# Cross-attention softmax denominators: one quad of each head summed by VectorE, with its neighbours' shares moved between GpSimd and TensorE

## The reference

```python
h, d, M = 16, 32, 8192
q = (layernorm(x) @ Wq + bq)        # 512 tokens, 16 heads of 32
k, v = ctx @ Wk + bk, ctx @ Wv + bv # 8192 keys
scores = einsum('nhd,mhd->hnm', q, k) / sqrt(32)
attn = softmax(scores, axis=-1)     # exp / sum over the 8192 keys
out = einsum('hnm,mhd->nhd', attn, v)
x = x + relu(out @ W1 + b1) @ W2 + b2
```

## Time and profile before

| | us |
|---|---|
| median of 3 runs | 1403.97 |
| the profiled execution, its own time | 1401.6 |
| its span, first to last instruction | 1399.8 |
| PE busy | 1330.5 (95%) |
| DVE busy | 1121.2 (80%) |
| ACT busy | 823.9 (59%) |
| POOL busy | 770.3 (55%) |

### The profile page before, as it was taken

The page is one execution under the profiler, slowest core; times in us unless marked ns, Lnnn a source line. Parts: engine busy times, 40 slices in busy tenths (PEclk is TensorE's granted clock), DMA queues, the critical chain, the costliest instruction groups (busy, mean ns, idle before and its releaser), DMA issues. The chain is left out here.

```text
span 1399.8 us, 39218 instructions
## 1 busy us (share of the span) xinstructions
PE 1330.5 (95%) x16678; PEld 709.8 (51%) x16678; DVE 1121.2 (80%) x1822; ACT 823.9 (59%) x1545; POOL 770.3 (55%) x304
## 2 busy tenths in 40 slices
PE   7999999998999999999999999999999998887898
PEld 4444444444655555555555555555555445555444
DVE  5678888887888888888888888888886764687875
ACT  4454444444777776777776777777777722475322
POOL 0321222221998988998898899889887001100111
PEclk9999999999999999999999999999999999999999
DMA  7567877787252122212212221221210030780000
GB/s 264 173 172 223 221 218 194 208 231 195 69 188 61 33 67 66 67 38 68 66 35 61 66 68 38 68 66 38 61 58 23 5 143 0 164 175 2 1 8 23
DMA packets 127794, 137.47 MB, mean 98 GB/s; under 512 B 44994, under 2 KB 108994, under 8 KB 125698
## 3 DMA queue, kind: packets, MB, share of 16 engines
q1 hardware_dynamic: 127620, 134.97, 33.9%
HBM read 75.69 MB, written 44.17 MB: 86 GB/s over the span
## 5 line engine op out<-in xcount | busy, mean ns | idle before, releaser
L1296 DVE TENSOR_REDUCE early<-attend_banks 128x1 f32<-128x512 f32 x952 | 611.8, 684 | 81.4 <-PE attend_banks L1041 76.0
L1260 ACT ACTIVATE attend_prob<-attend_banks 128x512 f32<-128x512 f32 x1024 | 535.9, 599 | 200.9 <-PE attend_banks L1078 198.7
L1438 POOL TENSOR_TENSOR early<-early,attend_prob 128x1024 f32<-128x1024 f32 x210 | 614.6, 2927 | 37.7 <-ACT attend_prob L1260 9.6
L1078 PE MATMUL attend_banks<-early,k_first 97*32 97x512 f16 x2560 | 262.1, 382 | 3.1 <-ACT attend_prob L1260 3.1
L1041 PE MATMUL attend_banks<-k_first,early 96*32 96x512 f16 x2272 | 236.0, 382 | 1.1 <-PEq L284 1.1
L1041 PE MATMUL attend_banks<-attend_k_rest,early 96*32 96x512 f16 x1536 | 158.2, 380 | 0.0
L1078 PE MATMUL attend_banks<-early,attend_k_rest 97*32 97x512 f16 x1536 | 154.3, 381 | 2.8 <-ACT attend_prob L1260 2.8
L1102 PE MATMUL attend_banks<-attend_prob,ones 128*32 128x128 f32 x3048 | 135.3, 272 | 3.6 <-DVE attend_recip L1308 3.6
L1091 PE MATMUL attend_banks<-attend_prob,wkv_area 128*32 128x512 f32 x1024 | 135.1, 592 | 0.0
L1091 PE MATMUL attend_banks<-attend_prob,attend_vh_odd 128*32 128x512 f32 x1024 | 133.7, 592 | 0.0
L502 POOL TENSOR_TENSOR project_w_whole<-project_grid,project_qscale 128x704 f32<-128x704 f32 x24 | 33.3, 1386 | 172.9 <-DVE project_grid L635 172.9
(11 more groups left out here) (212 smaller groups left out, 1816.5 us busy)
## 6 DMA issues: line engine op xcount, KB each, us to landing
v_scratch<-project_v SPq DMA_DIRECT2D x16, 1024.0 KB, 9.0
early<-in_ctx_dram SPq DMA_DIRECT2D x16, 768.0 KB, 6.3
k_first<-k_scratch SPq DMA_DIRECT2D x36, 256.0 KB, 3.4
k_scratch<-project_k_hi SPq DMA_DIRECT2D x64, 128.0 KB, 2.9
k_scratch<-project_k_lo SPq DMA_DIRECT2D x64, 128.0 KB, 3.0
attend_vh_odd<-v_scratch SPq DMA_DIRECT2D x8, 1024.0 KB, 4.9
wkv_area<-v_scratch SPq DMA_DIRECT2D x7, 1024.0 KB, 4.8
attend_k_rest<-k_scratch SPq DMA_DIRECT2D x24, 256.0 KB, 3.4
```

The costliest lines, as they stand in the source:

```text
L1078: last = nc.tensor.matmul(s_ps[c * HD:(c + 1) * HD, s_bank[n], :], key_rows[:, c * HD:(c + 1) * HD], q_stack[0:KROWS + 1, h, :], start=Tru ...
L1260: nc.scalar.activation(prob[:, q % PSLOTS, t, :], s_ps[:, s_bank[BT * q + t]], ACT.Exp, scale=SCALE).then_inc(p_ready, 1)
L1296: nc.vector.tensor_reduce(part_max[:, s, j, part:part + 1], pre_ps[:, bank], AX.X, ALU.max).then_inc(pre_read, 1)
L1438: nc.gpsimd.tensor_tensor(sums, sums, prob[:, q % PSLOTS, 0:n], ALU.add).then_inc(pool_summed, 1)
```

## The change

In each head but the last (15 of 16), quad 8 is no longer split between GpSimd and TensorE. VectorE sums its four tiles into `sum_dve` (128 x 512), in four quarters of 128 tokens. Each quarter is one `tensor_reduce` over the tile index: it reads 512 words per partition, the four that it adds up 2048 bytes apart, and writes 128. The quarters stand behind VectorE's maxima of tiles (9, 2), (10, 0), (10, 2) and (11, 0), where (q, j) is quad and tile. TensorE multiplies `sum_dve` with ones in the den step of quad 11, which stands in quad 13 of its program, after a wait on `quad_summed`. GpSimd skips quad 8 and takes three tiles of quads 6 and 10, where it took two. ScalarE waits for `quad_summed` before it writes quad 12 into the slot of quad 8.

```diff
+            sum_dve = sb("sum_dve", [P, T])
...
+            DVE_QUAD = 8
+            QUARTER_AT = {(DVE_QUAD + 1, 2): 0, (DVE_QUAD + 2, 0): 1, (DVE_QUAD + 2, 2): 2, (DVE_QUAD + 3, 0): 3}
+            ADDED_AT = DVE_QUAD + 3
+            def by_vector(h, q):
+                return q == DVE_QUAD and h < H - 1
             def pool_tiles(q):
-                return POOL_TILES if q < 2 or q % 2 else POOL_TILES - 1
+                if q == DVE_QUAD:
+                    return 0
+                return POOL_TILES if q < 2 or q % 2 or abs(q - DVE_QUAD) == 2 else POOL_TILES - 1
...
+                    if by_vector(h, q):
+                        return
+                    if by_vector(h, q - ADDED_AT + DVE_QUAD):
+                        pe.wait_ge(quad_summed, TT * (h + 1))
+                        for t in range(TT):
+                            nc.tensor.matmul(den_ps[t * HD:(t + 1) * HD, 0:P], ones[:], sum_dve[:, t * P:(t + 1) * P],
+                                             start=False, stop=False)
...
-                    last.then_inc(den_added, 1)
+                    last.then_inc(den_added, 2 if by_vector(h, q + 1) else 1)
...
+                        if q >= PSLOTS and by_vector(h, q - PSLOTS):
+                            act.wait_ge(quad_summed, TT * (h + 1))
...
+                def sum_quad(h, t):
+                    tokens = slice(t * P, (t + 1) * P)
+                    if t == 0:
+                        dve.wait_ge(p_ready, BT * (QUADS * h + DVE_QUAD + 1))
+                        wait(dve, den_added, QUADS * (h - 1) + ADDED_AT + 1)
+                    nc.vector.tensor_reduce(sum_dve[:, tokens], prob[:, DVE_QUAD % PSLOTS, :, tokens].rearrange("p n t -> p t n"),
+                                            AX.X, ALU.add).then_inc(quad_summed, 1)
...
                                 tile_max(s_of, part, j, TILES * h + TT * q + j,
                                          turn_of[(q, j)] % PRE_BANKS)
+                                if (q, j) in QUARTER_AT:
+                                    sum_quad(h, QUARTER_AT[(q, j)])
...
+                    if n == 0:
+                        return
...
-                                                ALU.add).then_inc(pool_summed, 1)
+                                                ALU.add).then_inc(pool_summed, 2 if pool_tiles(q + 1) == 0 else 1)
```

More of the change, by code:

```diff
@@ L887, in perceiver @@
             dve_summed = sem("dve_summed")
+            quad_summed = sem("quad_summed")
             o_in = [sem(f"o_in{k}") for k in range(DK)]
```

## The result

The changed kernel takes 1433.36 us (median of 6 runs, 1430.67 to 1433.85), against 1403.56 us before (6 runs): a ratio of 1.021, 95% interval 1.0198 to 1.0223. It is 29.8 us slower. The forecast was slower, 13.3 us, 1417 us; 1433 lies in the stated range, in the part that rival B was given.

A forecast was written before the change was run, and what follows sets the result against it. TensorE (PE) was taken to bound the kernel, VectorE close behind. Per head, 1.54 us of new waiting less 0.654 saved gives +0.89, x 15 = +13.3 us on 1403.97, so 1417 us; range 1405 to 1441.

The forecast's parts named there:

- rival B: VectorE's quarters: reading a new place with every word makes each 0.90 to 1.16 us, 1433 to 1448 us; chance 0.24.
- the 9.8 given: TensorE's program: three groups fewer per head, 0.654 us, save 9.8 us in 15 heads.
- the bank argument: Quads 10 to 12: TensorE waits until VectorE's maxima free the three banks, 4R - 1.04, or 1.54 us per head.
- The sign: Whole kernel: the change makes it slower, +0.89 us per head; slower was given 0.85.
- the covers: ScalarE's wait before quad 12 has 1.7 us of slack; GpSimd's later end is covered by 1.96 us without work.
- the claim that the first delay is absorbed and four are not all: TensorE's banks: one VectorE delay of 0.65 us is absorbed; four of them, two maxima apart, are not.
- the term R in part 2: VectorE's added work: one quarter, start to start, costs 0.645 us, bounded between 0.51 and 1.16.
- the interval of part 3: From pre tile (9, 2) to (12, 1): VectorE needs 6.34 + 4R us, with maxima at 0.645; TensorE alone needs 7.38.
- Case A: VectorE's quarters: each costs 0.51 to 0.8 us start to start, giving 1409 to 1426 us; chance 0.57.

The follow-up runs named there:

- e4: The change without VectorE's four sums, `sum_dve` set to zero once (quad 8 missing from the denominators): 1393.6 us, ratio 0.9942 to the kernel before.
- e1: The change with each quarter reading 512 words side by side instead of 2048 bytes apart (wrong sums): 1408.23 us, ratio 1.0042 to the kernel before.
- e6: The kernel before with the four quarters added, their sum unused, GpSimd and TensorE sharing tiles as before: 1435.69 us, ratio 1.0217 to the kernel before.
- e9: The change with each quarter reading four places 512 bytes apart inside one tile, instead of 2048 bytes apart (wrong sums): 1431.11 us, one run.
- e10: The change with each quarter reading three tiles in turn, 384 words instead of 512, the fourth tile left out: 1399.16 us, one run.
- e3: The change with each quarter reading two tiles in turn, word by word, 2048 bytes apart, writing 256 words (half the sum missing): 1403.6 us, one run.
- e2: The change with each quarter reading two neighbouring words, then stepping 2048 bytes, eight words added into one (wrong denominators): 1408.14 us, one run.
- e8: The kernel before with GpSimd taking three tiles of quad 2 instead of two, no work for VectorE: 1399.6 us, ratio 0.9966 to the kernel before.
- e11: The kernel before with GpSimd taking three tiles of quads 2 and 8, no work for VectorE: 1402.73 us, ratio 1.0001 to the kernel before.
- e8b: The kernel of e8 run again beside e11 on the same chip: 1399.25 us, ratio 0.9971 to the kernel before.

## Why the prediction was right and wrong

**Right: what bounds, and where the wait falls.** TensorE's program bounds the attention; three groups less are worth 8.3 us (e4) of the 9.8 given. PE waits in front of pre tiles of quads 10 to 12 in the head shown. With the prices of a maximum and a quarter measured, the bank argument gives the head's length within 0.1 us in nine kernels (the change, e1 to e6, e9, e10). The sign, the covers (no wait of ACT for the quarters, GpSimd not late in the change) and the claim that the first delay is absorbed and four are not all held.

GpSimd did as forecast. Its pause before quad 9 is there (the second row), and its pause at a head's end is 2.83 us (the third) where it was 1.96, since the head is longer.

```profile
722.97 3.47 POOL L1474 TENSOR_TENSOR early<-early,attend_prob 128x1536 f32<-128x1536 f32 x1 [0.17 <-POOL early L1474]
727.24 13.20 POOL L1474 TENSOR_TENSOR early<-early,attend_prob 128x1536 f32<-128x1536 f32 x4 [0.80 <-ACT attend_prob L1283]
753.61 3.47 POOL L1470 TENSOR_TENSOR early<-attend_prob 128x1536 f32<-128x1536 f32 x1 [2.83 <-issue]
```

**Wrong: the term R in part 2, the cost of a quarter.** "I choose 0.645, because the operation, the count and the word size are those of the nearest row, and only the step differs." The step was the thing that mattered: 1083 ns recorded, and R = 0.99 where R was put at 0.645. That alone is 4 x 0.345 = 1.38 us per head too little.

**Also wrong: 0.645 for a maximum, in the interval of part 3.** It was read from eight maxima with pauses among them (5.16 / 8); maxima that wait for nothing follow each other at 0.60. The interval holds eight, so it was 8 x 0.045 = 0.36 us too long. The two errors have opposite signs. What is left is 1.02 us per head, x 15 = 15.3 us.

By the rows a head of the change is 1.88 us longer, 28.2 us in 15 heads, where the forecast had 13.3. The other 1.6 of the 29.8 us are not divided up: the profiled executions show 0.4 us at the attention's start (PE's first pre tile at 343.8 instead of 343.4) and 3 us in the last stages, where executions of one and the same kernel differ by 4 us (below).

On its own condition, a quarter as fast as its nearest row, the forecast was too high: e1 has +0.24 us per head, 3.6 us in 15 heads, and +6.3 us between the medians, against 13.3. Case A, the likeliest by the text, would have come out at its lower end (1409) or under it.

A slip that changes nothing: GpSimd's adds of quads 9 to 15 are 5 x 3.62 + 2 x 2.51 = 23.1 us, not 23.0.

Rival B was the case that came, at the lower end of its price (0.90 to 1.16, 1433 to 1448), and its chance, 0.24, was too low. That its lower end is right to 1 us is partly luck: 4 x 0.90 + 8 x 0.645 and 4 x 0.99 + 8 x 0.60 are the same sum. That the range holds 1433 is owed to the half of B in it, not to the mechanism that was forecast. The text took a sentence of the Trainium skill (Vector Engine (DVE) Microarchitecture Reference, section 5.2) on a source alternating between two places as the nearest thing to four tiles. e3 bears that sentence out for two places, and the change shows that it doesn't carry to four. The same section's rule on words that come in pairs agrees with e2 (676 ns). Its figure of 1.73 ns per column for a source that hops each element is near the 1.82 ns per word measured here; the estimate of 1438 us from it was nearer than the forecast.

## What to carry to other kernels

Where a full engine gets work from another one, write the wait as an interval: what the helper must do between two points that the buffers tie together, less what the bound engine has to do there. The slack per head (6 us here) did not decide; that VectorE needs 5.98 us where TensorE needs 7.38 did, so that it could take on 1.4 us there and no more. A duration taken from a row holds for that row's access pattern: for a `tensor_reduce` that reads four places in turn, word by word, allow 1.8 ns per word instead of 1.0, or read at most three places, or pairs (measured at steps of 2048 bytes, four places also at 512). A start-to-start time is to be taken from operations that wait for nothing: the mean over a merged row can hold pauses. When one tile more fits into a pause of the engine that already does the work (e8), it can beat bringing in a new one; a second tile (e11) did not fit.

## What was not expected of the hardware

The limit between three places in turn (1.14 ns per word at steps of 2048 bytes) and four (1.82, the same at steps of 512 and 2048 bytes).

The last stages move the time by themselves. From the last reciprocal to the end the profiled executions take between 281.8 us (e3) and 287.1 (e6), though the program there is the same in all. Two executions of the same kernel, e8 and e8b, have their last reciprocals at 1113.6 and 1113.7 us, and take 282.4 and 286.7 us from there, so that their spans are 1396.0 and 1400.4 us. Their granted clocks differ in places, most in these 50 us (columns as in rows 1, the granted clock is the number behind the five busy times):

```profile
1250.00:1300.00 50.00, 38.81 (x362) 25.71 (x359) 36.55 (x98) 26.06 (x59) 0.00 (x0) 0.97 0.01 1
```

```profile
1250.00:1300.00 50.00, 39.02 (x371) 26.11 (x370) 35.38 (x94) 25.62 (x61) 0.00 (x0) 0.90 0.01 1
```

The longer one was granted 0.90 of full speed there, the shorter 0.97. That the clock makes all of the 4.3 us is not shown. The change's profiled execution has 287.0 us there, that of the kernel before 283.8, so 3.2 of the 31.8 us between their spans lie where both have the same program, and such a difference also comes without the change.
